# Rebuilt setup and engine orders in a four-layer conditional block kernel, with short bf16 matmuls whose results nobody reads

## The reference

```python
# layer 0, a graph attention, for the two directions d
cond = A.sum(-1); vb = A @ w_bias + b_bias            # A = adj[:, :, :20, :] or its transpose
aff = where(cond > 0, q @ k / sqrt(8), -9e15) + vb     # 16 heads, 20 keys
output = output + (softmax(aff) @ kv) projected by Wout
x = x + relu(output)
# layer 1, attention (causal) and MLP, each modulated by the condition
mod = silu(condition) @ Wada + bada
xm = layernorm(x, g, be) * (1 + scale) + shift
x = x + gate * _attention(xm);  x = x + gate * MLP(xm)
# layer 2: two modulated MLPs.  layer 3: as layer 1, without the causal mask
```

## Time and profile before

| | us |
|---|---|
| median of 3 runs | 629.04 |
| lowest and highest | 628.34, 631.07 |
| the profiled execution | 627.14 |
| its span in the trace | 625.3 |
| PE, DVE, ACT, POOL busy | 524.5, 463.3, 350.3, 328.0 |

### The profile page before, as it was taken

The page is one execution under the profiler, slowest core; times in us unless marked ns, Lnnn a source line. Parts: engine busy times, 40 slices in busy tenths (PEclk is TensorE's granted clock), DMA queues, the critical chain, the costliest instruction groups (busy, mean ns, idle before and its releaser), DMA issues.

```text
span 625.3 us, 24101 instructions
## 1 busy us (share of the span) xinstructions
PE 524.5 (84%) x10598; PEld 357.3 (57%) x10598; DVE 463.3 (74%) x1031; ACT 350.3 (56%) x576; POOL 328.0 (52%) x324
## 2 busy tenths in 40 slices
PE   2287886778799997878898998999889989988897
PEld 1154555645567674646656664666657655665675
DVE  7988677788878738766787497588995857689930
ACT  1037452233579667665674666436456976867842
POOL 4406110333546888764673452234537689856573
PEclk9999788787799996978999998598979999979999
DMA  8610353012315305124443421321232243032421
GB/s 299 248 27 18 72 157 77 22 41 56 90 35 156 121 16 150 52 58 127 145 106 99 127 74 44 92 73 42 92 105 69 65 125 102 22 114 61 124 68 68
DMA packets 35256, 56.91 MB, mean 91 GB/s; under 512 B 14672, under 2 KB 19664, under 8 KB 35152
## 3 DMA queue, kind: packets, MB, share of 16 engines
q1 hardware_dynamic: 34688, 54.42, 30.2%
q10 hardware_dynamic: 432, 0.94, 0.4%
q0 software_dynamic: 32, 0.01, 0.3%
HBM read 42.37 MB, written 3.54 MB: 73 GB/s over the span
## 4 chain that ended last, share of the span: by engine, by line
PE 43%; DVE 22%; POOL 16%; issue 12%; ACT 5%; DMA 1%; POOLq 0%; DVEq 0%
PE work L1059 8%; PE work L1010 7%; PE work L1025 6%; POOL x L650 4%; DVE stats L882 4%; PE work L967 3%; PE work L1002 3%; POOL rstd L641 3%; PE work L1068 3%; POOL xm L655 3%; PE work L970 2%; PE work L1038 2%; POOL x L646 2%; PE work L975 2%; DVE mx L850 2%
## 5 line engine op out<-in xcount | busy, mean ns | idle before, releaser
L722 ACT ACTIVATE xn<-x,nmr,rstd 128x128 f32<-128x128 f32 x192 | 78.3, 483 | 39.7 <-POOL nmr L643 39.7
L850 DVE TENSOR_REDUCE mx<-work 128x32 f32<-128x1024 f32 (+1 forms) x64 | 65.0, 1016 | 43.6 <-PE work L1010 41.5
L1059 PE MATMUL work<-xm,w_layer 128*128 128x512 f32 x176 | 95.2, 652 | 2.4 <-POOL xm L655 1.6
L1068 PEld LDWEIGHTS work<-w_layer,prob 128*128 128x128 f32 x704 | 81.7, 192 | 10.8 <-issue 5.6
L1010 PE MATMUL work<-kbd,q_gate 32*32 32x80 f32 (+1 forms) x4096 | 77.7, 273 | 11.8 <-issue 5.6
L650 POOL TENSOR_TENSOR x<-x,q_gate 128x512 f32<-128x512 f32 x48 | 60.7, 1270 | 49.7 <-DVE q_gate L899 48.5
L1068 PE MATMUL work<-w_layer,prob 128*128 128x128 f32 x704 | 84.7, 277 | 2.3 <-ACT prob L727 1.3
L655 POOL TENSOR_TENSOR xm<-turned_in,mod 128x512 f32<-128x512 f32 x48 | 50.6, 1055 | 66.0 <-DVE turned_in L894 65.9
L1010 PEld LDWEIGHTS work<-kbd,q_gate 32*32 32x32 f32 x4096 | 66.7, 112 | 28.0 <-issue 13.7
L713 ACT ACTIVATE prob<-prob 128x640 f32<-128x640 f32 (+1 forms) x64 | 56.5, 895 | 42.2 <-DVE prob L852 41.9
L727 ACT ACTIVATE prob<-work,first 128x512 f32<-128x512 f32 x88 | 58.6, 685 | 35.4 <-PE work L1059 34.9
(11 more groups left out here) (124 smaller groups left out, 804.3 us busy)
## 6 DMA issues: line engine op xcount, KB each, us to landing
q_gate<-gates_out SPq DMA_DIRECT2D x192, 128.0 KB, 2.8
vbd<-v_ev SPq DMA_DIRECT2D x128, 72.0 KB, 2.5
kbd<-in_adj SPq DMA_DIRECT2D x8, 704.0 KB, 6.6
edge_rep<-spread SPq DMA_DIRECT2D x32, 80.0 KB, 2.3
turned_in<-in_x_tok SPq DMA_DIRECT2D x8, 256.0 KB, 3.2
out_x<-x SPq DMA_DIRECT2D x8, 256.0 KB, 2.0
turned_in<-in_x_feat SPq DMA_DIRECT2D x7, 256.0 KB, 4.3
w_layer<-in_weights SPq DMA_DIRECT2D x2, 768.0 KB, 14.3
```

Source lines behind the costliest of these rows:

```text
L722: act.activation(xn[s][:, t], x[s][:, t], ACT.Identity, scale=rstd[s][:, t:t + 1], bias=nmr[s][:, t:t + 1]).then_inc(xn_ready[s], 1)
L850: dve.tensor_reduce(mx[s][:], src, AX_X, ALU.max).then_inc(dve_step[s], 1)
L1059: pe.matmul(bank(s, f"h{j}.{u}"), w[UP[j]][:, 0, u * D:(u + 1) * D], xm[s][:], start=True, stop=True).then_inc(filled[s], 1)
L1068: last = pe.matmul(bank(s, f"y{a}")[:, t * D:(t + 1) * D], hT[s][u][:, t * P:(t + 1) * P], w[DOWN[a]][:, u], start=(u == 0 and t == 0), st ...
```

## The change

**Setup.** The clears of prob and vbd go from DVE and POOL to ACT (eight ACTIVATE Copy of a zero column: 128x64x12 for prob and 128x2304 for vbd, three of them ahead of `qs`, the others between the first stages). ACT also evacuates the mod products with scale and bias in one instruction each; DVE is left with one scalar_tensor_tensor for the four blocks that have a gain, and with small products of biases that are worked out once. The mod weights now lie in w_layer[2] and w_layer[3], the gates in w_layer[1], silu in the gate half of q_gate of stream 3; the real layer weights are loaded after the mod and gate products (SP stages `weights`). SP waits for `first_loaded` before it issues chunk 1's x and adjacency, and for chunk 0's adjacency before the mod weights. The edges of chunk 0 are worked out on DVE alone, from the integers. The silu steps move from the head of DVE's list into the setup's stages.

**Stats.** DVE's memset and the two small operations after the aggregation become one tensor_reduce (the negated mean); variance plus epsilon goes to POOL as a third small operation ahead of the power.

**Unread matmuls.** PE gets 128x128 bf16 matmuls with 512 columns of the identity, whose results the next real matmul in the same bank overwrites: 6 at the start, 2 before each of the six mod products, 2 before each of the first four rowsums, 1 before each half of the graph attentions' scores (32 in all).

**Orders.** All five MERGE strings are new.

```diff
+WARM = {'start': 6, 'mod': 2, 'rowsum': 2, 'graph scores 0': 1, 'graph scores 1': 1}
...
-SETUP = {"tensor": MODS + GATES, "vector": CLEARS + MODS + GATES, "scalar": GATES[1:], "gpsimd": [],
-         "sync": [("gates", 0, 0)]}
+SETUP = {"tensor": MODS + GATES, "vector": SILU + [MODS[j] for j in GAINED] + GATES, "scalar": SILU + CLEARS + MODS + GATES[1:],
+         "gpsimd": [], "sync": [("weights", 0, 0), ("gates", 0, 0), ("weights", 1, 0)]}
...
-    "tensor": ("014441424444030103133202030312013032102012033110313003212201332001013032330021300131202310303001"
+    "tensor": ("001110244144440404201301003010101210120031332130213130303223103131033121023023013103213012330323"
...
             load_adj(0)
+            sp.wait_ge(first_loaded, 16)
             load_x(1)
             load_adj(1)
...
+            sp.wait_ge(adj_loaded[0], 16)
+            sp.dma_start(w_layer[2][:], t_in["modw"][:, 0:6 * D]).then_inc(modw_loaded, 16)
+            sp.dma_start(w_layer[3][:], t_in["modw"][:, 6 * D:18 * D]).then_inc(modw_loaded, 16)
...
+                if kind == "weights":
+                    if a == 0:
+                        sp.wait_ge(setup_filled, BEFORE_MODS + NBLK + 2)
+                        for layer in (2, 3):
+                            sp.dma_start(w_layer[layer][:], t_in[f"weights{layer}"]).then_inc(w_loaded[layer], 16)
+                    else:
+                        sp.wait_ge(gates_stored, 16)
+                        sp.dma_start(w_layer[1][:], t_in["weights1"]).then_inc(w_loaded[1], 16)
...
-            pool.memset(vbd[0][:], 0.0).then_inc(pool_clear, 1)
...
-                    pool.wait_ge(veps_ready[s], count(c, NBLK, a + 1))
+                    pool.wait_ge(dve_step[s], count(c, OWN_STEPS, OWN["aggr", a]))
+                    pool.tensor_tensor(veps[s][:], mv[s][:, :, 1], eps[EPS[a]][:], ALU.add).then_inc(pool_step[s], 1)
...
+                act.activation(flat, zeros.broadcast_to(shape), ACT.Copy).then_inc(act_clear, 1)
...
+                    if a in GAINED:
+                        act.activation(scale, ps[:, 0:B], ACT.Identity, scale=vec("gain", k), bias=gained_scale[:, k:k + 1])
+                        act.activation(shift, ps[:, B:2 * B], ACT.Identity, bias=gained_shift[:, k:k + 1]).then_inc(mod_ready, 1)
...
-                if kind == "clear":
-                    if a < NS:
-                        dve.memset(prob[a][:, NG - 1 if a == NS - 1 else 0:, :, NONGT:], 0.0).then_inc(dve_clear, 1)
-                    else:
-                        dve.memset(vbd[a - NS + 1][:], 0.0).then_inc(dve_clear, 1)
...
+                    dve.scalar_tensor_tensor(out=shift, in0=mod_bank[a][:, 0:B], scalar=vec("gain_bias", k), in1=shift,
+                                             op0=ALU.mult, op1=ALU.add).then_inc(gain_ready, 1)
...
+                            dve.tensor_tensor(grid, ints, wb.unsqueeze(1).broadcast_to([P, BT * S, L]), ALU.mult
+                                              ).then_inc(adj_scaled, 1)
...
-                    own(("stats", a))
-                    dve.memset(wait_slot[:], 0.0)
                     for t in range(T):
+                        dve.wait_ge(dve_step[s], count(c, OWN_STEPS, OWN["stats", a] - T + t + 1))
                         dve.bn_aggr(mv[s][:, t], stats[s][:, t]).then_inc(dve_step[s], 1)
                     own(("aggr", a))
-                    dve.tensor_scalar(neg_mean[s][:], mv[s][:, :, 0], -1.0, None, ALU.mult)
-                    dve.tensor_scalar(veps[s][:], mv[s][:, :, 1], EPS[a], None, ALU.add).then_inc(veps_ready[s], 1)
+                    dve.tensor_reduce(neg_mean[s][:], mv[s][:, :, 0:1], AX_X, ALU.add, negate=True).then_inc(mean_ready[s], 1)
...
+            def keep_warm(to, kind):
+                for _ in range(WARM.get(kind, 0)):
+                    pe.matmul(to, ident16[:], ident16[:].unsqueeze(1).broadcast_to([P, T, P]), start=True, stop=True)
...
+                    warm = ("graph scores" if a < 2 else "scores") + f" {pair}"
+                    if WARM.get(warm):
+                        await_bank(pe, c, f"S{pair} a{a}")
+                        keep_warm(work[s][:, 0], warm)
```

More of the change, by code:

```diff
@@ L139, with runs @@
 MODS = [("mod", n, 0) for n in range(NBLK)]
-CLEARS = [("clear", n, 0) for n in range(2 * NS - 1)]
+CLEARS = [("clear", n, 0) for n in range(3, 2 * NS)]
+SILU = [("silu", 0, 0)]
 GATES = [("gates", n, 0) for n in range(2)]
-SETUP = {"tensor": MODS + GATES, "vector": CLEARS + MODS + GATES, "scalar": GATES[1:], "gpsimd": [],
-         "sync": [("gates", 0, 0)]}
+SETUP = {"tensor": MODS + GATES, "vector": SILU + [MODS[j] for j in GAINED] + GATES, "scalar": SILU + CLEARS + MODS + GATES[1:],
+         "gpsimd": [], "sync": [("weights", 0, 0), ("gates", 0, 0), ("weights", 1, 0)]}
 def lanes(engine):
-    streams = [[st for c in range(s, NCH, NS) for st in chunk_stages(c) if st[0] in PARTS[engine]] for s in range(NS)]
+    def runs(st):
+        return st[0] in PARTS[engine] and not (engine == "gpsimd" and st[0] == "edges" and st[2] in EDGE_DVE)
+    streams = [[st for c in range(s, NCH, NS) for st in chunk_stages(c) if runs(st)] for s in range(NS)]
     return streams + [SETUP[engine]]
@@ L162 @@
[L162 to L169, removed]
@@ L276, in build @@
         neg_half = sb("neg_half", [P, T])
-        wait_slot = sb("wait_slot", [P, 1])
+        eps = {value: sb(f"eps_{k}", [P, T]) for k, value in enumerate(sorted(set(EPS)))}
         zero_col = sb("zero_col", [P, 1])
@@ L472, in width, with await_mod, adj_count @@
             return NONGT if a < 2 else S
+        def await_mod(eng, j):
+            eng.wait_ge(mod_ready, j + 1)
+            eng.wait_ge(gain_ready, sum(g <= j for g in GAINED))
+        def adj_count(c, k):
+            return sum(2 for b in range(c % NS, c, NS) if b not in EDGE_DVE) + k
         def modw(j):
@@ L599, in _ @@
             pool.memset(neg_half[:], -0.5)
+            for value, tile in eps.items():
+                pool.memset(tile[:], value)
             pool.memset(zero_col[:], 0.0).then_inc(const_step, 1)
@@ L924, in stage @@
                 if kind == "mod":
+                    if a >= 2:
+                        await_mod(pe, a - 2)
+                    keep_warm(mod_bank[a], "mod")
                     if a == 0:
@@ L988, in stage @@
                             pe.wait_ge(masks_step, MASKS)
-                    await_bank(pe, c, f"S{pair} a{a}")
+                    if not WARM.get(warm):
+                        await_bank(pe, c, f"S{pair} a{a}")
                     def tile(t, g):
@@ L1016, in stage @@
                     name = f"O{pair} a{att}"
+                    if WARM.get("values"):
+                        await_bank(pe, c, name)
+                        keep_warm(bank(s, name), "values")
                     pe.wait_ge(turned[s], count(c, NATT * PAIRS, a + 1))
@@ L1053, in stage @@
                     j, u = divmod(a, UNITS)
+                    if u == 0 and WARM.get("hidden"):
+                        await_bank(pe, c, f"h{j}.{u}")
+                        keep_warm(bank(s, f"h{j}.{u}"), "hidden")
                     if u == 0:
@@ L1079, in get @@
         return np.asarray(inputs[name])
-    cols = [get(name).reshape(k, P).T for name, k in VECTORS]
+    own_bias = {"scale_bias": [], "shift_bias": []}
+    for j in MOD_COL:
+        layer, second = BLOCKS[j][1], j % 2
+        if layer == 3:
+            parts = [get(f"L3_cond_{n}_b") for n in (("g2", "b2") if second else ("g1", "b1"))]
+        else:
+            ada = get("L1_cond_bada" if layer == 1 else "L2_cond_ada_b").reshape(6, D)
+            parts = [ada[3 * second + k] for k in (1, 0)]
+        own_bias["scale_bias"].append(parts[0])
+        own_bias["shift_bias"].append(parts[1])
+    own_bias["gain"] = [get(n) for n in ("L1_cond_g1", "L1_cond_g2", "L3_cond_ln1_g", "L3_cond_ln2_g")]
+    own_bias["gain_bias"] = [get(n) for n in ("L1_cond_be1", "L1_cond_be2", "L3_cond_ln1_b", "L3_cond_ln2_b")]
+    cols = [(np.stack(own_bias[name]) if name in own_bias else get(name).reshape(k, P)).T for name, k in VECTORS]
     own = get("L0_cond_W_self")
```

227 lines of the change are left out of this document (129 added, 98 removed), and 6 rows, old and new, of the table VECTORS.

## The result

| | kernel before | changed kernel |
|---|---|---|
| median, us | 628.69 (4 runs, 620.24 to 631.07) | 596.11 (4 runs, 591.77 to 601.08) |
| ratio | | 0.950, 95% interval 0.935 to 0.965 |
| span of the profiled execution, us | 625.3 | 599.3 |
| PE, DVE, ACT, POOL busy | 524.5, 463.3, 350.3, 328.0 | 519.8, 426.7, 365.9, 330.8 |

The change saves 33 us, 5%. Two later measurements of the changed kernel, on other chips, gave ratios of 0.945 and 0.954. The profiled execution of the changed kernel is the slowest of its four (601.08 us), so a second trace of it, from run c0_after (span 596.5), is named where the two differ.

A forecast was written before the change was run, and what follows sets the result against it. No engine was full: PE was busy 84% of the span and 43% of the chain. Span 625.3 - 13 (front) + 0.5 (unread matmuls) - 2 (stats) = 610.8, with 1.8 and 1.9 us added 614.5; own range 606 to 621, overall 599 to 630.

The forecast's parts named there:

- The front: Setup up to the first score unit: that unit 20 us earlier, at about 35; worth -13 us (-20 to -8).
- The first rowsum: PE's setup, chunk 0: near the upper clock level, its first instructions at half the old duration each.
- ACT's clears: Setup on ACT: 0.95 us for 768 elements and 2.55 for 2304, eight in all 14 us.
- from the first mod product to the first score unit: End of the setup: mod products begin at 29.5 us, chunk 0's first score unit starts at about 35.
- The orders past the front: New instruction orders after the setup: not priced from rows, taken as 0, with -6 to +6 us.
- What a microsecond at the lower level costs: Graph stages, 75 us at the lower level: 0.4 of PE's busy time lost, 22 us, 11 on the path.
- The unread matmuls: Score units' 32: +3.5 us of cost, half on the path, and -3 given back by the clock; net +0.5.
- the unread matmuls stand on the path: Rival, setup and score units: all 58 exposed at 0.43 us, no clock gained, 24.9 us, time 639; chance 0.08.
- the clock holds too: Rival, score units: unread matmuls bring back all 11 us on the path, front's debt 4 us more hidden; 602; chance 0.17.
- Idle time and the clock: Skill's rule that long idle gaps drop the clock; the busy 104 to 108 us stretch was held against it.
- Stats: Layer norm's small operations: DVE's relief -5 us, POOL's added work +3, net -2 (-5 to +3).
- The sum: Whole kernel: span 625.3 - 13 + 0.5 - 2 = 610.8 us, median 614.5.

The follow-up runs named there:

- e13: The changed kernel without its 58 unread matmuls, run as the base for two others on one chip: 592.72 us, ratio 0.938 to the kernel before.
- e10: The kernel before with the new orders and none of the new code, so no unread matmuls: 605.81 us against 631.03, ratio 0.959.
- e5: The changed kernel's code, unread matmuls included, with the five order strings of the kernel before: 639.28 us against 633.01, ratio 1.013.
- e12: The changed kernel's code with the old orders up to the point reached at 200 us and the new ones from there: 621.93 us against 631.03, ratio 0.984.
- e3: The kernel before with 32 unread matmuls, one ahead of each half of the graph attentions' scores: 631.59 us against 633.01, ratio 0.998.

## Why the prediction was wrong

**The front, step by step.** The identity was there at 4.0 (forecast 3.9), the six unread matmuls took 2.72 us (2.6), the first `self` evacuation began at 11.89 (12), DVE's edges at 13.70 (13.5), the mod products at 30.68 (29.5), all right. The first rowsum was to run near the upper level of the clock and didn't, which cost little (1.91 us). ACT's clears were cheaper than the slope from smaller operations, 0.84 and 2.12 us for 0.95 and 2.55. One step was mis-sized: from the first mod product to the first score unit it took 9.7 us, not 5.5. The first two products ran at the lower level again (1.20 us for the first four instructions, 0.61 for the later ones), behind PE's wait of 9.06 us for silu; that is 1 us or so. The unread matmuls between them aren't the rest: without any it takes 9.0 (30.16 to 39.15 in e13). I take it for the alternation of PE's pair, ACT's two instructions and DVE's one in each bank, which no run took apart. So the first score unit came 15 us sooner instead of 20. The lead at 25% of the work was 15 us in this trace, 8 and 10 in two later ones, all within the term's -20 to -8. But it isn't the rebuilt setup's alone, as I had it: the old code under the new orders, whose first score unit starts at 47.00, is 7 us ahead there too, and the new code under the old ones 2.

**The orders past the front** is the step that failed. I wrote that I can't price them from rows, took 0, and bounded it by 6 us of placement. They are the largest term: 26 us together with those of the front (e10), 18 us the later ones alone, with the same start (e5 against e12), and 20 us of PE's busy time in the late stretch. A part of what was needed stood in the rows. The earlier trace rows had the low digits of slices 24 to 29, and I used them only to ask what unread matmuls might give back; the digits 6, 7, 8 and 7 of slices 15, 17, 18 and 35 I left out, though some 28 of the 107 us at the lower level lie there. I had looked for placement gains in waits, and most of it came as busy time at a higher clock. How much an order list raises the clock I still couldn't say ahead of a run.

**What a microsecond at the lower level costs** was the second mis-sized term. I took 0.4 of busy time and 0.51 of that on the path, 0.2 together. Between the two kernels of the late stretch it is 19.7/39 = 0.5: PE is busy 89% of the time there and nothing of the saved busy time turned into idle time, so the average share of the chain (43/84) doesn't hold. At 0.5 the 75 us of the earlier trace rows would be worth 37 us and not 11. The price isn't the same everywhere: among the 17 executions of the kernel before on one chip it is only 0.14 (last section).

**The unread matmuls** were put at +0.5. In the kernel before that is what they are worth (e3). In the changed one the score units' 32 cost 9 us, and the setup's nothing. The hidden half that I granted the score units isn't there, and neither are the 3 us that the clock was to give back (0.943 with them, 0.939 without). That the new orders keep PE supplied and have already brought that clock is my reading, not shown. The rival "the unread matmuls stand on the path" was right for the 32 and its price per matmul (0.43) too high. The rival "the clock holds too" came nearest with 602, but not by its mechanism: the clock rose by the orders, in a kernel without any unread matmul (e10).

**Idle time and the clock.** The Trainium skill, in "TensorE: Matmul & The Clock Gate", section "HAM oscillation — how this bites in real kernels", ties the lower level to long idle gaps. The traces agree more than I had granted: 13 of the 17 falls in the kernel before stand behind an idle time of 1 us or more, that at 386.7 behind 2.01 us. So does the stretch from 104 to 108 us that I had held against the rule: it belongs to a low stretch that began at 103.4, behind 1.45 us of idle time from 100.6 on. What the rule doesn't give is why the lower level then lasts through 17 us in which PE is busy.

**Stats** were forecast at -2 and came as 0 to -8. **The sum**: orders -26, setup and stats code under them -13 (0.959 to 0.937), unread matmuls +6 to +9, together -30 to -33 for -33 measured. It holds for this sequence only: under the old orders the same code, with the unread matmuls, is worth +8.

## What to carry to other kernels

Look at TensorE's granted clock by stretch first, and price the lower level by the busy time of a stretch in which TensorE is the bound; here a kernel pair gave half of the time at that level. Then go to the start of each low stretch and look at what TensorE did just before: here it had mostly been idle for 1 to 2 us, and an instruction order with the same idle time in smaller pieces had the higher clock. One timeline doesn't show which of its features matters; a count over all falls of the clock does. Unread matmuls beside score units cost their full time (the same kernel without them there is faster, 589.5 against 597.5). A lead won at the start is kept only under orders that go with it: with unread matmuls, the new code was worth -3 to -9 us under the new orders and +8 under the old.

## What the runs showed of the hardware

- The granted clock falls mostly behind idle time of PE of 1 us or more (13 of 17 falls in the kernel before, 7 of 10 in e10, from 60 us on), and can then stay at the lower level while PE is busy, here for 16.76 of 17.00 us (386.7 to 403.7 us in the kernel before), more than half of it on small tiles.
- The clock column prints 1.00 for the first 35 us of the kernel before, although a 512-column fp32 instruction takes 0.95 us there and 0.51 afterwards: before its first record the column tells nothing, the durations do.
- Executions of one and the same kernel differ by what they got of the clock: six of the changed kernel on one chip had mean clocks of 0.933 to 0.955 and spans of 608.4 to 592.5, about 0.5 us for each microsecond at the lower level. But 17 of the kernel before on the same chip, with clocks of 0.871 to 0.923, give 0.14.
- A small fp32 operation on DVE can last until a POOL operation beside it is over: the mask operation that took 1.73 us under POOL's memset, from 3.29 to 5.02 with the memset's end at 4.99, takes 0.17 in the changed kernel, at the same place without it. The two operations before it, from 3.01 and 3.07, took 0.15 and 0.18 under the same memset, so not every one is held up.
